# Running sums of a linear attention over pairs of even and odd tokens, five heads in 32 bits and eleven in two halves

## The chip, the cores and the metric
The kernel runs on one core of a Trainium2 chip. TensorE (PE) does the matmuls, VectorE (DVE) and ScalarE (ACT) the work on elements, GpSimd (POOL) small operations and gathers, SyncE (SP) issues most DMA. The metric is the time of one execution on the device in microseconds (us), as a median of several runs.

## What is computed
Two layers on x of 16 sequences, 256 tokens each, 128 wide. Each layer normalises x and adds to it an attention and a feed-forward branch. The first layer has a causal linear attention of 16 heads of width 8 and a mixture of 8 experts, of which each token uses 2. The second has a linear attention without a causal order and a gated feed-forward branch that mixes each token with the one before it. The change concerns mainly the causal attention:

```
def step(carry, qkv):
    K_sum, KV = carry
    q_t, k_t, v_t = qkv
    K_sum = K_sum + k_t
    KV = KV + k_t[..., :, None] * v_t[..., None, :]
    num = jnp.einsum('bhd,bhde->bhe', q_t, KV)
    den = jnp.maximum(jnp.einsum('bhd,bhd->bh', q_t, K_sum), EPS)
    return ((K_sum, KV), num / den[..., None])
```

q and k have gone through a rotation by position and phi(x) = elu(x) + 1. So each token needs, for each head, the sum over all tokens up to it of a product of k (8 numbers) with v and a one (9 numbers): 16 x 9 x 8 = 1152 running sums for a token.

## The kernel before
**Tiles.** A tile is 128 tokens, one on each partition; there are 32, numbered i. A sequence b has two tiles, i = 2b (r = 0, its tokens 0 to 127) and i = 2b + 1 (r = 1, tokens 128 to 255). A sequence is also called a pair here, since it is a pair of tiles.

**The running sums.** `phi` (DVE) makes q and k of a pair. `attn_outer` (DVE) and `attn_keys` (ACT) write the 1152 products of a tile into `outer`. A float32 matmul is slow, so `attn_high` (ACT) rounds the products to a narrower format, `fp32r`, and `attn_low` (DVE) makes the rest; both halves go to PE. `attn_cumsum` (PE) multiplies them with a triangle of ones (`tri_r`), which gives the running sum within the tile; for the second tile of a pair the first tile's products are multiplied with a matrix of ones (`ones_r`) too. The 1152 columns lie in three banks of PSUM, of 5, 5 and 6 heads (360, 360 and 432 columns): 6 matmuls in a first tile, 12 in a second. `attn_apply` (DVE) multiplies the result with q into `cq`, `attn_sums` (DVE) adds over the 8 numbers, and after the second tile `attn_reciprocal` and `attn_divide` (DVE) give y, which PE transposes and projects.

**The order.** Each engine runs its own list of instructions, and semaphores tie them together. The running sums are woven into the 71 steps of the experts: in one step PE transposes the tokens of block j + 2, multiplies the first weights of block j + 1 and the second of block j; ACT takes copies and the gelu. The table `SUMS_AT` gives the step after whose first part the sums of tile i stand on PE: two steps from tile to tile, three at one place, four after the tiles 20 and 25 (`READY_AT`), where DVE also runs `combine` and the second layer's moments for four tiles. One pair has mostly four expert steps. On DVE the order within a tile is written out in `tile`: apply(i), low(i+1), outer(i+2), sums(i), and behind a second tile reciprocal, divide and phi(b+2). So the halves for the next tile are ready before DVE does the sums of this one. POOL gathers the tokens of the expert blocks by indirect DMA (`gather`, six blocks ahead of its count, held back until PE has transposed the block four before), and later the results of the experts (`gather_y`).

**The rest.** Before the experts lie the projections of the first layer (8 groups of four tiles) and the routing. After them comes the second layer in 8 groups of four tiles (`group_tensor`, `group_vector`, ...); in the first five groups DVE also combines the attention's and the experts' results for a later group. `mix` (DVE) adds the token before to each token: columns 0 to 255 of `xT2` to columns 1 to 256.

## Time and profile before
| | |
|---|---|
| median of 3 runs | 368.7 us (367.78 to 368.82) |
| the profiled execution | 367.48 us, of which the span of its instructions is 365.7 us |
| PE busy | 347.7 us (95%) |
| DVE busy | 317.6 us (87%) |
| ACT busy | 276.1 us (75%) |
| POOL busy | 204.3 us (56%) |
| granted clock of PE | 0.999 of full speed |

The profile is of one execution; the time outside its span is 1.8 us. Busy shares are averages over very different stages: the first layer's projections and the routing up to about 68 us, the experts with the running sums up to about 280 us, then the second layer. What binds is read stage by stage.

### The profile page before, as it was taken

The page shows a single profiled execution, that of the slowest core. Times are in us where ns is not written, and L with a number is a line of the kernel's source. Part 1 is how long each engine was busy: PE and PEld are TensorE (multiplying, and loading weights), DVE is VectorE, ACT ScalarE, POOL GpSimd, SP SyncE. Part 2 cuts the span into 40 slices and gives each one's busy share as a digit, 9 for nine tenths or more (in the row PEclk, how much of TensorE's full clock was granted, in tenths as well). Part 3 has the DMA queues.
Part 4 walks back from the last instruction along what each step waited for, and adds up shares of the span by engine and source line. Part 5 has one row for each costly group of instructions (what it writes and reads, how often), then busy time and mean ns, then how long its engine had stood idle before and what let it go on. Part 6 is the DMA issues. An engine that isn't in the chain of part 4 may idle for free.

```text
span 365.7 us, 9318 instructions
## 1 busy us (share of the span) xinstructions
PE 347.7 (95%) x2534; PEld 299.9 (82%) x2534; DVE 317.6 (87%) x623; ACT 276.1 (75%) x774; POOL 204.3 (56%) x239
## 2 busy tenths in 40 slices
PE   7999988799899999999999899999999899999986
PEld 2788534499799999999999799989989688788875
DVE  3998799559989999999699979998996799998665
ACT  3887967777686877787878767787895987778752
POOL 3899118844234465756665648675857448883110
PEclk9999999999999999999999999999999999999999
DMA  6842848555355555655654554756642102221112
GB/s 182 217 124 74 325 192 234 173 149 134 108 133 137 139 143 146 170 139 150 175 143 135 152 161 129 186 150 152 148 115 70 31 2 57 57 61 29 30 29 59
DMA packets 45521, 47.00 MB, mean 129 GB/s; under 512 B 6928, under 2 KB 33712, under 8 KB 45216
## 3 DMA queue, kind: packets, MB, share of 16 engines
q1 hardware_dynamic: 40288, 36.88, 33.6%
q0 software_dynamic: 4320, 8.86, 11.5%
q10 hardware_dynamic: 864, 0.67, 0.7%
q8 instruction: 23, 0.38, 0.5%
q14 instruction: 26, 0.21, 0.2%
HBM read 32.88 MB, written 13.50 MB: 127 GB/s over the span
## 4 chain that ended last, share of the span: by engine, by line
PE 76%; DVE 14%; issue 3%; ACT 3%; DMA 2%; ACTq 1%; DVEq 0%
PE banks L546 16%; PE banks L534 14%; PE banks L674 6%; PE banks L675 6%; PE banks L330 3%; PE banks L983 3%; PE banks L1010 2%; PE banks L299 2%; PE banks L524 2%; PE banks L1039 2%; PE banks L321 2%; PE banks L1019 2%; PE banks L993 2%; PE banks L1057 2%; DVE cq L686 2%
## 5 line engine op out<-in xcount | busy, mean ns | idle before, releaser
L468 POOL DMA_INDIRECT xg<-xn_rows,slot_tok x71 | 74.8, 1053 | 74.2 <-PE banks L524 61.7
L563 ACT ACTIVATE xT<-banks,b1T 128x128 f32<-128x128 f32 x284 | 81.1, 371 | 15.4 <-PE banks L534 14.7
L546 PE MATMUL banks<-w_sb,xT 128*128 x568 | 79.6, 283 | 0.0
L485 POOL DMA_INDIRECT qk_exp<-expert_rows,ranki x64 | 63.7, 996 | 21.6 <-issue 17.9
L534 PE MATMUL banks<-xgT,w 128*128 128x128 f32 x568 | 75.3, 276 | 0.0
L546 PEld LDWEIGHTS banks<-w_sb,xT 128*128 128x128 f32 x568 | 69.3, 192 | 1.2
L534 PEld LDWEIGHTS banks<-xgT,w 128*128 128x128 f32 x568 | 69.0, 192 | 0.0
L686 DVE TENSOR_TENSOR cq<-banks,phi 128x360 f32<-128x360 f32 (+1 forms) x96 | 47.4, 548 | 19.1 <-PE banks L675 18.9
L652 ACT CAST high<-outer 128x1152 fp32r<-128x1152 f32 x32 | 37.1, 1158 | 21.6 <-DVE outer L641 21.2
L658 DVE TENSOR_TENSOR low<-outer,high 128x1152 fp32r<-128x1152 f32 x32 | 43.3, 1352 | 3.2 <-ACT high L652 3.2
L695 DVE TENSOR_REDUCE sums<-cq 128x144 f32<-128x1152 f32 x32 | 42.9, 1341 | 0.0
L641 DVE TENSOR_TENSOR outer<-phi,qkv 128x1024 f32<-128x1024 f32 x32 | 38.7, 1213 | 0.0
L674 PE MATMUL banks<-high,tri_r 128*128 128x360 f32 (+1 forms) x96 | 35.1, 365 | 1.1 <-DVE low L658 1.1
L675 PE MATMUL banks<-low,tri_r 128*128 128x360 f32 (+1 forms) x96 | 32.4, 337 | 0.0
L299 PE MATMUL banks<-zeros_bf 128*128 128x512 bf16 x111 | 28.9, 404 | 1.7 <-DVE zeros_bf L1529 1.0
L291 ACT ACTIVATE xn<-x_sb,shift,rstd 128x128 f32<-128x128 f32 x64 | 26.5, 486 | 0.3 <-POOL shift L279 0.3
L572 ACT COPY ye<-banks 128x128 f32<-128x128 f32 x71 | 19.4, 273 | 9.6 <-PE banks L546 9.1
L524 PE MATMUL banks<-cst,xg 128*128 128x128 f32 x71 | 19.6, 276 | 3.8 <-issue 1.8
L934 POOL TENSOR_TENSOR outer<-outer,x_sb 128x512 f32<-128x512 f32 x7 | 8.9, 1272 | 22.7 <-DVE outer L929 22.6
L555 ACT COPY xgT<-banks 128x128 f32<-128x128 f32 x71 | 19.0, 268 | 3.3 <-PE banks L524 2.5
L299 PEld LDWEIGHTS banks<-zeros_bf 128*128 128x128 bf16 x111 | 10.5, 103 | 12.8 <-issue 2.5
L275 POOL TENSOR_TENSOR rstd<-ve,mhalf 128x4 f32<-128x4 f32 x16 | 19.3, 1207 | 1.3
(205 smaller groups left out, 702.7 us busy)
## 6 DMA issues: line engine op xcount, KB each, us to landing
w<-in_L_ffn_W SPq DMA_DIRECT2D x71, 256.0 KB
expert_rows<-ye SPq DMA_DIRECT2D x71, 64.0 KB
expert_rows<-x_sb SPq DMA_DIRECT2D x2, 2048.0 KB, 10.6
x_sb<-in_L_attn_x SPq DMA_DIRECT2D x8, 256.0 KB, 4.3
xn_rows<-xn SPq DMA_DIRECT2D x8, 256.0 KB, 2.3
w_sb<-in_L_ffn_W SPq DMA_DIRECT2D x8, 256.0 KB, 4.5
out<-outer SPq DMA_DIRECT2D x7, 256.0 KB, 2.3
xg<-xn_rows,slot_tok POOLq DMA_INDIRECT x71
```

Of the source, the lines that this page charges most:

```text
L299: nc.tensor.matmul(ps[bank], zeros_bf[:, :], zeros_bf[:, :].unsqueeze(1).broadcast_to([P, 4, P]), start=True, stop=True)
L468: pool.indirect_dma_start(out=xg[n][:, :], out_offset=None, in_=xn_dram, in_offset=bass.IndirectOffsetOnAxis(ap=slot_tok[:, j:j + 1], axis ...
L485: pool.indirect_dma_start(out=y_moe[:, i, k, :], out_offset=None, in_=y_dram, in_offset=bass.IndirectOffsetOnAxis(ap=ranki[:, 0, k, i:i + ...
L534: last = nc.tensor.matmul(ps[3 + p][:, c * P:(c + 1) * P], w1[n][:, c * P:(c + 1) * P], xgT[p][:, :], start=True, stop=True)
L546: last = nc.tensor.matmul(y, hidT[p][:, c, :], w2_sb[:, ds(e * NC + c, 1), :], start=False, stop=(c == NC - 1))
L563: last = nc.scalar.activation(hidT[p][:, c, :], ps[3 + p][:, c * P:(c + 1) * P], ACT.Gelu_apprx_tanh, bias=b1T[:, ds(e * NC + c, 1)])
L641: nc.vector.tensor_tensor(outer_of(r)[:, :, 0:DH, :], k.unsqueeze(2).broadcast_to([P, H, DH, DH]), vv.unsqueeze(3).broadcast_to([P, H, DH, ...
L658: nc.vector.tensor_tensor(low[n], outer[r], high[n].bitcast(f32), ALU.subtract).then_inc(low_ready, 1)
L674: nc.tensor.matmul(o, w[:, :], high[at][:, cols], start=(m == 0), stop=False)
L675: last = nc.tensor.matmul(o, w[:, :], low[at][:, cols], start=False, stop=(m == len(parts) - 1))
L686: last = nc.vector.tensor_tensor(cq4[:, lo:hi, :, :], ps[n][:, 0:(hi - lo) * E9 * DH].rearrange("p (h e d) -> p h e d", e=E9, d=DH), q[:, ...
L695: nc.vector.tensor_reduce(sums[:, r, :, :], cq4, AX.X, ALU.add).then_inc(sums_ready, 1)
```

## The change
Tokens are laid out differently: partition p of a first tile holds token 2p of its sequence, partition p of a second tile token 2p + 1. The sums over a pair then need only one product of ones and sums of two tokens: DVE adds the products of the two tiles first (`attn_pair`), and only this sum is split and sent to PE. For the odd tokens the triangle includes the diagonal (`tri_r`), for the even ones it doesn't (`tri_x`), and what the even token adds itself is q . k times v, which POOL computes in five operations (`attn_own`) and DVE adds to the sums (`attn_add_own`). The first five heads (360 columns, `whole`) aren't split: they go to PE as one float32 matmul. Loads and stores of tokens now move two neighbouring tokens (1 KB) at a time; `mix` gets four instructions instead of two; in the second layer PE takes the blocks in swapped order (`block_of`). ACT copies three more 128x128 matrices at the start. A few semaphores are shared by the layers, which changes no order.

```
@@ constant_table @@
-        put(name, a.reshape(2, P, DH).transpose(1, 0, 2).reshape(P, -1))
+        put(name, a.reshape(P, -1))
...
+    def by_tile(a, b, n):
+        return a.rearrange("(b p r) d -> p b (r d)", p=P, r=2)[:, b:b + n, :]
+
+    def in_pairs(a):
+        return a.rearrange("p (b r) d -> p b (r d)", r=2)
...
-    high = [sbuf(f"high{n}", [P, HED], f32r)[:, :] for n in range(3)]
-    low = [sbuf(f"low{n}", [P, HED], f32r)[:, :] for n in range(3)]
-
-    def kept(r, p):
-        return 2 if r else p
+    HEADS = ((0, 5), (5, 10), (10, H))
+    WHOLE = HEADS[0][1] * E9 * DH
+    whole = [sbuf(f"whole{n}", [P, WHOLE])[:, :] for n in range(2)]
+    high = [sbuf(f"high{n}", [P, HED - WHOLE], f32r)[:, :] for n in range(2)]
+    low = [sbuf(f"low{n}", [P, HED - WHOLE], f32r)[:, :] for n in range(2)]
...
@@ attn_keys, attn_outer @@
-            act.wait_ge(high_ready, b * 2 - 1 + r)
-            act.wait_ge(low_ready, b * 2 - 1 + r)
+            act.wait_ge(high_ready, b)
+            act.wait_ge(low_ready, b)
+            act.wait_ge(pair_ready, b)
+            act.wait_ge(whole_ready, b)
...
-    def attn_high(act, b, r, p):
-        i = b * 2 + r
-        act.wait_ge(outer_ready, i + 1)
-        act.wait_ge(den_ready, i + 1)
-        if from_(b, 2 - r):
-            act.wait_ge(cum_ps, b * 2 - (0 if r else 2))
-        nc.scalar.copy(high[kept(r, p)], outer[r]).then_inc(high_ready, 1)
-    def attn_low(v, b, r, p):
-        v.wait_ge(high_ready, b * 2 + r + 1)
-        n = kept(r, p)
-        nc.vector.tensor_tensor(low[n], outer[r], high[n].bitcast(f32), ALU.subtract).then_inc(low_ready, 1)
-    HEADS = ((0, 5), (5, 10), (10, H))
+    def attn_pair(v, b, p):
+        v.wait_ge(outer_ready, 2 * b + 2)
+        v.wait_ge(den_ready, 2 * b + 2)
+        if b >= 2:
+            v.wait_ge(cum_ps, 2 * b - 2)
+        nc.vector.tensor_tensor(outer[0][:, WHOLE:], outer[0][:, WHOLE:], outer[1][:, WHOLE:], ALU.add).then_inc(pair_ready, 1)
+        nc.vector.tensor_tensor(whole[p], outer[0][:, 0:WHOLE], outer[1][:, 0:WHOLE], ALU.add).then_inc(whole_ready, 1)
+    def attn_high(act, b, p):
+        act.wait_ge(pair_ready, b + 1)
+        if b >= 2:
+            act.wait_ge(cum_ps, 2 * b - 2)
+        nc.scalar.copy(high[p], outer[0][:, WHOLE:]).then_inc(high_ready, 1)
+    def attn_low(v, b, p):
+        v.wait_ge(high_ready, b + 1)
+        nc.vector.tensor_tensor(low[p], outer[0][:, WHOLE:], high[p].bitcast(f32), ALU.subtract).then_inc(low_ready, 1)
+    def attn_own(pool, b, p):
+        pool.wait_ge(phi_ready, b + 1)
+        if b >= 2:
+            pool.wait_ge(own_used, b - 1)
+        nc.gpsimd.tensor_tensor(own_qk[:, :], phib[p][:, 0, 0:D], phib[p][:, 0, D:2 * D], ALU.mult).then_inc(own_part, 1)
+        q = own_qk[:, :].rearrange("p (h d) -> p h d", d=DH)
+        n = 4 * b + 1
+        for half in (DH // 2, DH // 4):
+            pool.wait_ge(own_part, n)
+            nc.gpsimd.tensor_tensor(q[:, :, 0:half], q[:, :, 0:half], q[:, :, half:2 * half], ALU.add).then_inc(own_part, 1)
+            n += 1
+        pool.wait_ge(own_part, n)
+        nc.gpsimd.tensor_tensor(own_dot[:, :], q[:, :, 0], q[:, :, 1], ALU.add).then_inc(own_part, 1)
+        pool.wait_ge(own_part, n + 1)
+        pool.wait_ge(ones_ready, 1)
+        nc.gpsimd.tensor_tensor(own[p][:, :, :], own_dot[:, :].unsqueeze(2).broadcast_to([P, H, E9]),
+                                qkv3[:, 2 * b, 2 * D:NW].rearrange("p (e h) -> p h e", h=H), ALU.mult).then_inc(own_ready, 1)
+    def attn_add_own(v, b, p):
+        v.wait_ge(own_ready, b + 1)
+        v.wait_ge(sums_ready, 2 * b + 1)
+        nc.vector.tensor_tensor(sums[:, 0, :, :], sums[:, 0, :, :], own[p][:, :, :], ALU.add).then_inc(own_used, 1)
     def attn_cumsum(pe, b, r, p):
...
         i = b * 2 + r
         if from_(i, 1):
             pe.wait_ge(cq_ready, i)
-        pe.wait_ge(low_ready, i + 1)
-        parts = [(tri_r, kept(r, p))] + ([(ones_r, kept(0, p))] if r else [])
+        pe.wait_ge(low_ready, b + 1)
+        pe.wait_ge(whole_ready, b + 1)
+        w = tri_r if r else tri_x
         for n, (lo, hi) in enumerate(HEADS):
             cols = slice(lo * E9 * DH, hi * E9 * DH)
             o = ps[n][:, 0:(hi - lo) * E9 * DH]
-            for m, (w, at) in enumerate(parts):
-                nc.tensor.matmul(o, w[:, :], high[at][:, cols], start=(m == 0), stop=False)
-                last = nc.tensor.matmul(o, w[:, :], low[at][:, cols], start=False, stop=(m == len(parts) - 1))
+            if n == 0:
+                nc.tensor.matmul(o, tri_whole[r][:, :], whole[p], start=True, stop=True)
+                continue
+            cols = slice(cols.start - WHOLE, cols.stop - WHOLE)
+            nc.tensor.matmul(o, w[:, :], high[p][:, cols], start=True, stop=False)
+            last = nc.tensor.matmul(o, w[:, :], low[p][:, cols], start=False, stop=True)
...
@@ attn_reciprocal @@
         v.wait_ge(sums_ready, 2 * b + 2)
+        v.wait_ge(own_used, b + 1)
...
+    OWN_AT = [max(SUMS_AT[2 * b] - 3, 0) for b in range(B)]
...
@@ mix @@
-            t = mix_t[p][m].rearrange("p (b t) -> p b t", t=T)
-            last = nc.vector.scalar_tensor_tensor(out=t, in0=xT2_of(p)[:, :, 0:T], scalar=one_mu[:, m:m + 1],
-                                                  in1=t, op0=ALU.mult, op1=ALU.add)
+            for lo, to in ((P + 1, 0), (0, P)):
+                t = mix_t[p][m].rearrange("p (b t) -> p b t", t=T)[:, :, to:to + P]
+                last = nc.vector.scalar_tensor_tensor(out=t, in0=xT2_of(p)[:, :, lo:lo + P], scalar=one_mu[:, m:m + 1],
+                                                      in1=t, op0=ALU.mult, op1=ALU.add)
...
@@ load_x: save, save_out alike @@
-                sp.dma_start(x_sb[:, tiles, :],
-                             x_in.rearrange("b t d -> (b t) d").rearrange("(n p) d -> p n d", p=P)[:, tiles, :]
+                sp.dma_start(in_pairs(x_sb[:, tiles, :]), by_tile(x_in.rearrange("b t d -> (b t) d"), 2 * g, 2)
...
@@ block.scalar @@
+                    nc.scalar.copy(tri_x[:, :], passing("tri_excl"))
+                    for r, name in enumerate(("tri_excl", "tri_incl")):
+                        nc.scalar.copy(tri_whole[r][:, :], passing(name))
...
+                if i % 2 and i + 1 < NT:
+                    attn_high(act, (i + 1) // 2, (i + 1) // 2 % 2)
...
-                if i + 2 < NT:
-                    attn_keys(act, i // 2 + 1, i % 2, 1 - i // 2 % 2)
-                    attn_high(act, i // 2 + 1, i % 2, 1 - i // 2 % 2)
+                if i % 2 == 0 and i + 2 < NT:
+                    for r in range(2):
+                        attn_keys(act, i // 2 + 1, r, 1 - i // 2 % 2)
...
+            for r in range(2):
+                attn_keys(act, 0, r, 0)
             def first():
-                for r in range(2):
-                    attn_keys(act, 0, r, 0)
-                attn_high(act, 0, 0, 0)
-            def second():
-                attn_high(act, 0, 1, 0)
+                attn_high(act, 0, 0)
...
@@ block.gpsimd @@
+                if j in OWN_AT:
+                    attn_own(pool, OWN_AT.index(j), OWN_AT.index(j) % 2)
...
@@ block.vector, tile @@
-                if i + 1 < NT:
-                    attn_low(v, (i + 1) // 2, (i + 1) % 2, (i + 1) // 2 % 2)
-                if till(b, B - 2):
-                    attn_outer(v, b + 1, r, 1 - p)
-                attn_sums(v, i, r)
-                if r == 1:
+                if r == 0:
+                    if b + 1 < B:
+                        phi(v, b + 1, 1 - p)
+                        for t in range(2):
+                            attn_outer(v, b + 1, t, 1 - p)
+                        attn_pair(v, b + 1, 1 - p)
+                    attn_sums(v, i, r)
+                else:
+                    attn_add_own(v, b, p)
+                    attn_sums(v, i, r)
+                    if b + 1 < B:
+                        attn_low(v, b + 1, 1 - p)
                     attn_reciprocal(v, b)
                     attn_divide(v, b)
-                if r == 1 and till(b, B - 3):
-                    phi(v, b + 2, p)
-            for b in range(2):
-                phi(v, b, b)
+            phi(v, 0, 0)
             for r in range(2):
                 attn_outer(v, 0, r, 0)
-            attn_low(v, 0, 0, 0)
+            attn_pair(v, 0, 0)
+            attn_low(v, 0, 0)
```

What stands in the engines' lists, at two places of the stage with the experts and one on POOL.

DVE, one pair of tiles in the steady part (`cq<-banks,phi` is apply, `low` and `outer` are as above, `sums<-cq` is the reduction, `rden` the reciprocal). Before:

```order
L686 TENSOR_TENSOR cq<-banks,phi 128x360 x2
L686 TENSOR_TENSOR cq<-banks,phi 128x432
L658 TENSOR_TENSOR low<-outer,high 128x1152
L641 TENSOR_TENSOR outer<-phi,qkv 128x16x64
L695 TENSOR_REDUCE sums<-cq 128x144
L686 TENSOR_TENSOR cq<-banks,phi 128x360 x2
L686 TENSOR_TENSOR cq<-banks,phi 128x432
L658 TENSOR_TENSOR low<-outer,high 128x1152
L641 TENSOR_TENSOR outer<-phi,qkv 128x16x64
L695 TENSOR_REDUCE sums<-cq 128x144
L700 RECIPROCAL rden<-sums 128x32
L708 SCALAR_TENSOR_TENSOR y_tok<-rden,sums 128x256
```

In the changed kernel, again from a first tile's apply on (`outer<-outer` is the sum of the tiles' products for eleven heads, `whole<-outer` for five, `sums<-sums,by_turn` adds what the even tokens add themselves):

```order
L742 TENSOR_TENSOR cq<-banks,phi 128x360 x2
L742 TENSOR_TENSOR cq<-banks,phi 128x432
L635 SCALAR_TENSOR_TENSOR phi<-qk_exp,qkv 128x512
L664 TENSOR_TENSOR outer<-phi,qkv 128x16x64 x2
L673 TENSOR_TENSOR outer<-outer 128x792
L674 TENSOR_TENSOR whole<-outer 128x360
L751 TENSOR_REDUCE sums<-cq 128x144
L742 TENSOR_TENSOR cq<-banks,phi 128x360 x2
L742 TENSOR_TENSOR cq<-banks,phi 128x432
L712 TENSOR_TENSOR sums<-sums,by_turn 128x144
L751 TENSOR_REDUCE sums<-cq 128x144
L686 TENSOR_TENSOR low<-outer,high 128x792
```

The two outer products, the pair's sums and phi (which stood behind the division) all stand in the first tile's part; the one split, `low`, stands at the end of the second tile's part, behind its reduction, and is what the next pair's first matmuls wait for.

PE, the running sums of a second tile between the experts' matmuls. Before:

```order
L674 MATMUL banks<-high,tri_r 128x360
L675 MATMUL banks<-low,tri_r 128x360
L674 MATMUL banks<-high,ones_r 128x360
L675 MATMUL banks<-low,ones_r 128x360
L674 MATMUL banks<-high,tri_r 128x360
L675 MATMUL banks<-low,tri_r 128x360
L674 MATMUL banks<-high,ones_r 128x360
L675 MATMUL banks<-low,ones_r 128x360
L674 MATMUL banks<-high,tri_r 128x432
L675 MATMUL banks<-low,tri_r 128x432
L674 MATMUL banks<-high,ones_r 128x432
L675 MATMUL banks<-low,ones_r 128x432
```

In the changed kernel (`tri_whole` is the float32 triangle):

```order
L727 MATMUL banks<-whole,tri_whole 128x360
L730 MATMUL banks<-high,tri_r 128x360
L731 MATMUL banks<-low,tri_r 128x360
L730 MATMUL banks<-high,tri_r 128x432
L731 MATMUL banks<-low,tri_r 128x432
```

Twelve matmuls in fp32r become four, and one in float32 is added; a first tile has the same five with `tri_x` instead of its six.

POOL, in the changed kernel, where before there were only gathers (L487 is the gather of an expert block's tokens):

```order
L487 DMA xg<-xn_rows,slot_tok 128x128 x4
L694 TENSOR_TENSOR own_qk<-phi 128x128
L700 TENSOR_TENSOR own_qk<-own_qk 128x16x4
L700 TENSOR_TENSOR own_qk<-own_qk 128x16x2
L703 TENSOR_TENSOR own_dot<-own_qk 128x16
L706 TENSOR_TENSOR own<-own_dot,qkv 128x144
L487 DMA xg<-xn_rows,slot_tok 128x128 x4
```

The five operations stand behind every fourth gather, one chain for each pair.

## Rows read from the trace of the kernel before
In the first group the columns are the stretch and its length, then the busy us (and the number of instructions) of PE, PEld, DVE, ACT and POOL, PE's granted clock, and the DMA's share and GB/s. In rows in order of time the columns are start, us, engine, line, operation, and in brackets the idle time before and what ended it; x3 means three instructions merged.

**Rows 1.** Windows of 10 us: experts with sums, and second layer.
```profile
110.00:120.00 10.00, 10.00 (x81) 9.45 (x80) 9.67 (x12) 7.54 (x25) 3.99 (x4) 1.00 0.55 147
...
310.00:320.00 10.00, 9.99 (x66) 8.12 (x66) 9.93 (x28) 7.82 (x16) 8.51 (x10) 1.00 0.20 52
```

**Rows 2.** Timeline of PE, running sums of tiles 9 and 10.
```profile
129.79 0.41 PE L674 MATMUL banks<-high,tri_r 128*128 128x360 f32 x1
...
131.97 0.23 PE L544 MATMUL banks<-bias,ones_bf 128*128 x1
...
136.07 0.41 PE L674 MATMUL banks<-high,tri_r 128*128 128x360 f32 x1
...
137.21 0.23 PE L544 MATMUL banks<-bias,ones_bf 128*128 x1
```

**Rows 3.** The chain that ended last: one float32 matmul of 512 columns.
```profile
296.63 0.86 PE banks L1019 x2
```

**Rows 4.** Timeline of DVE, one tile and what follows.
```profile
108.08 1.49 DVE L686 TENSOR_TENSOR cq<-banks,phi 128x360 f32<-128x360 f32 x3 [0.99 <-PE banks L675]
109.49 1.35 DVE L658 TENSOR_TENSOR low<-outer,high 128x1152 fp32r<-128x1152 f32 x1
110.76 1.21 DVE L641 TENSOR_TENSOR outer<-phi,qkv 128x1024 f32<-128x1024 f32 x1
111.89 1.34 DVE L695 TENSOR_REDUCE sums<-cq 128x144 f32<-128x1152 f32 x1
113.27 0.35 DVE L700 RECIPROCAL rden<-sums 128x32 f32<-128x32 f32 x1
...
114.00 0.68 DVE L616 SCALAR_TENSOR_TENSOR phi<-qk_exp,qkv 128x512 f32<-128x512 f32 x1
```

**Rows 5.** Timeline, where DVE and PE wait for each other.
```profile
74.65 0.41 PE L674 MATMUL banks<-high,tri_r 128*128 128x360 f32 x1
...
75.98 1.49 DVE L686 TENSOR_TENSOR cq<-banks,phi 128x360 f32<-128x360 f32 x3 [3.34 <-PE banks L675]
...
91.57 1.35 DVE L658 TENSOR_TENSOR low<-outer,high 128x1152 fp32r<-128x1152 f32 x1
...
93.07 0.40 PE L674 MATMUL banks<-high,tri_r 128*128 128x360 f32 x1 [1.12 <-DVE low L658]
```

**Rows 6.** Timeline of PE, first matmuls of tiles 12 and 30.
```profile
148.12 0.41 PE L674 MATMUL banks<-high,tri_r 128*128 128x360 f32 x1
...
270.53 0.41 PE L674 MATMUL banks<-high,tri_r 128*128 128x360 f32 x1
```

**Rows 7.** Timeline of DVE behind tile 20, combine and moments.
```profile
206.38 2.17 DVE L828 SCALAR_TENSOR_TENSOR x_sb<-qk_exp,sel,x_sb 128x128 f32<-128x128 f32 x8
...
209.49 0.38 DVE L268 BATCH_NORM_AGGREGATE mv<-stats 128x2 f32<-128x6 f32 x4
```

**Rows 8.** Timeline, copies on ACT near the start, and the experts' start.
```profile
16.04 0.30 ACT L1329 CAST tri_r<-cq 128x128 fp32r<-128x128 f32 x1
...
16.24 0.30 ACT L1330 CAST ones_r<-cq 128x128 fp32r<-128x128 f32 x1
...
18.25 1.19 PE L321 MATMUL banks<-w_in,xT 128*128 128x136 f32 x8 [0.64 <-ACT xT L338]
...
70.09 1.15 ACT L652 CAST high<-outer 128x1152 fp32r<-128x1152 f32 x1
```

**Rows 9.** Timeline of POOL and DVE in the second layer.
```profile
306.31 1.27 POOL L934 TENSOR_TENSOR outer<-outer,x_sb 128x512 f32<-128x512 f32 x1
...
307.12 1.03 DVE L888 SCALAR_TENSOR_TENSOR qkv<-qkv 128x512 f32<-128x512 f32 x1
...
309.74 0.20 POOL L277 TENSOR_TENSOR minus<-mv,rstd 128x4 f32<-128x4 f32 x1
...
335.90 0.66 DVE L888 SCALAR_TENSOR_TENSOR qkv<-qkv 128x512 f32<-128x512 f32 x1
```

**Rows 10.** Timeline of DVE, the two instructions of mix.
```profile
311.77 1.44 DVE L880 SCALAR_TENSOR_TENSOR qkv<-qkv,one_mu 128x512 f32<-128x512 f32 x2
```

More of the change, by code:

```diff
@@ L1056, in nd_tensor @@
         for n in range(GT):
[L1057 removed]
+            last = nc.tensor.matmul(nd_bank[:, n, 0:DA], phi_q[:, block_of(n)], kvm[:, n // 2, :],
                                     start=True, stop=True)
@@ L1399, in _ @@
                   even, odd,
-                  first=first, second=second, last=last)
+                  first=first, last=last)
             groups(act, group_scalar)
```

72 lines of the change are left out of this document (40 added, 32 removed).

## The prediction, written before the changed kernel was run
> **What bounds the kernel now.** I read the busy time in stretches first. In the stage of the experts PE has no idle time (10.00 of 10 us) and DVE nearly none (9.67); in the second layer both are full (9.99 and 9.93) [rows 1]. So little is free on two engines, and the question is which chain closes last. The timeline of PE gives the terms of a pair: 2.18 us for the sums of a second tile (129.79 to 131.97), 4.10 for two expert steps (to 136.07), 1.14 for the sums of a first tile (to 137.21) [rows 2]. In this stage PE waits for hardly anything, and what DVE produces is ready before PE asks: PE sets the pace, and DVE is some tenths of a us short of it.
>
> **PE's part.** A float32 matmul of 512 columns takes 0.86 us, recorded in two [rows 3]; for 360 columns that is 0.61. Six fp32r matmuls take 1.14 us for 2 x 1152 columns, so the 720 columns replaced took 0.36, and a tile now costs 1.14 - 0.36 + 0.61 = 1.39 us. A pair costs 2.78 instead of 3.32: PE gains 0.54 of work per pair. This is all that the change can give while PE binds.
>
> **DVE's part.** From the starts in one tile: apply 1.41, low 1.27, outer 1.13, reduction 1.27 (1.34 with its tail); reciprocal and divide 0.73 together, phi 0.68 with its tail [rows 4]. Phi with 512 elements (0.68) and low with 1152 (1.35) give 1.05 ns an element, so 792 elements take 0.97 alone and 0.90 in a row of work, 360 take 0.46, and the 144 of the own part some 0.25. Removed per pair: two lows, 2.54. Added: 0.90 + 0.46 + 0.25 + 0.97 = 2.58. DVE has nothing to gain. What counts is the new order. Low stands last in the second tile's part, PE's next sums wait for it, and the next thing DVE can do beyond reciprocal and divide is the apply that waits for those sums. Before, low stood directly behind apply, and outer and reduction covered PE's sums. Where the two wait for each other, PE starts 0.15 us after low has ended (91.57 + 1.35 to 93.07), and apply starts 1.33 us after the first of six matmuls [rows 5]; with the float32 one this is 1.33 + 0.25 = 1.58.
>
> The loop of one pair, from the first matmul of its first tile to that of the next pair's: sums 1.58, apply 1.41, phi 0.68 (outer waits for its end), outer 1.13 and 1.21 (the sum of the pair waits for the second), pair 0.90, whole 0.46, reduction 1.27, apply 1.41, own 0.25, reduction 1.27, low 0.97, to PE 0.15. Together 12.7 us. PE's own way round is 12.05 - 0.54 = 11.5, where 12.05 is the pair from 136.07 to 148.12 [rows 2, 6]. So the bound moves from PE's work to this loop, 0.65 over the pair of before; DVE stands about 0.85 in it (1.58 less the 0.73 of reciprocal and divide), and PE waits 1.2.
>
> What could break this loop: keys on ACT. They now follow phi by one expert step, after PE has done the first tile's sums, one and a half steps and ACT one copy. By PE's terms that is 1.39 + 2.05 + 2.05 at most, and they end before DVE has done both outers (1.58 + 1.41 + 0.68 + 2.34 = 6.0). The split to high, 0.8 us on ACT, starts at about 7.0 and is needed at about 11.6. Both are hidden.
>
> **The sum over the stage.** Fifteen pairs lie between the first matmuls of tile 0 (74.65) and tile 30 (270.53): 195.9 us [rows 5, 6]. After: twelve at 12.7 = 152.4. Pair 7 has a fifth expert step, and PE binds: 11.5 + 2.05 = 13.6. Pair 12 (extra steps ahead of tile 26) has PE at 11.5 + 4.1 = 15.6, while combine falls into PE's time. Pair 10 has combine and moments inside the loop, 206.38 to 209.87 or 3.5 us [rows 7]: 12.7 + 3.5 = 16.2. Sum 197.8, +1.9 us. The last pair has no follower: PE's 0.5 less, 0.25 for the own part more, -0.25.
>
> **The ends.** Three more 128x128 copies on ACT at the start, 0.20 us each by two neighbours, stand ahead of the xT copy for which PE already waits 0.64: +0.6. At the experts' start the first gelu stands behind the keys and a high of 1.15 us on ACT, and the second behind another; now the keys are done earlier and one high of 0.84 is left [rows 8]. I take -0.7 (0.3 to 1.5).
>
> **POOL's own part.** Five operations per pair, in a stage where POOL only gathered. Where they run beside DVE a row of the second layer shows a price: a DVE instruction with both inputs in SBUF is issued at 307.12 while POOL adds 512 columns (306.31 to 307.58), and takes 1.03 us; with POOL idle the same line takes 0.66 at 335.90 [rows 9]. It gets through when POOL is done, 0.4 later. POOL's small operation takes 0.20 for 4 columns, the large one 1.27 for 512, so the five take about 0.46, 0.33, 0.26, 0.22 and 0.50: 1.8 us. The chain waits for phi, and behind phi DVE has four instructions with two SBUF inputs (outer, outer, pair, whole). If each of the first three POOL operations gets in between two of them and costs its length less 0.1, a pair loses 0.75 us; if POOL's chain falls into applies and reductions, with PSUM or a single input, it loses nothing. I take half, 0.35, as phi is what both wait for but POOL has a gather to issue first. In thirteen pairs in which DVE's loop binds: +4.5 us (0 to 9.8). The Trainium skill, "SBUF — State Buffer", section Who interferes with whom, states the rule: a DVE instruction with two SBUF inputs and a GpSimd instruction that reads SBUF shut each other out for the whole instruction. By that rule the trace's 0.4 us is what is to be expected; taken strictly for all that can meet, the sum would be near its upper end.
>
> **Second layer and DMA.** Two mix instructions of 512 elements take 1.44 us [rows 10]; four of 256 have the same elements and two more fixed parts, 0.68 - 512 x 1.05 ns = 0.14 alone and less in a row: +0.2 per mix. It counts where DVE is full, the first mix and five groups: +1.2. Loads and stores in 1 KB pieces move the same bytes with half the packets; only the first load and the last store aren't covered: -0.2 (0 to -0.6). The swapped blocks change no size.
>
> **Sum.** +1.9 - 0.25 + 0.6 - 0.7 + 4.5 + 1.2 - 0.2 = +7.1 us. The profiled execution took 367.5, so it would take 374.6; it lies 1.2 below the median of the runs shown, within their usual spread, and I add the sum to the median: 375.8 us.
>
> **The rivals.**
> (a) The loop holds, but POOL's chain doesn't meet DVE's: 375.8 - 4.5 = 371.3, range 369.8 to 373.5. For it: applies and reductions, which read PSUM or a single input, are 5.4 of the loop's 12.7 us, and with DVE's wait of 0.85 half of it is free for POOL. Against it: POOL's chain and the outer products both start on phi.
> (b) Faster. PE stays the bound, since DVE's loop is shorter than 12.05 us. Then fifteen pairs at 0.54 less give -8.1, with -0.25 - 0.7 + 0.6 + 1.2 - 0.2 the sum is -7.4: 361.3; with the loop halfway, at 11.8, about 365. The loop would have to be 0.65 shorter than by the rows, a quarter of all that is new on DVE. For it: PE binds now and loses work. Against it: the durations of apply, outer, reduction and low are measured ones.
> (c) About the same: the loop at 12.2 and no meeting: 368.7 +- 1.1.
> (d) POOL costs more, since each operation in the chain of five meets DVE, own part included, or POOL comes late with the gathers of the experts' tokens, which stand in its list between the chains. At 0.7 to 1.0 us a pair instead of 0.35 the thirteen pairs cost 9 to 13 instead of 4.5: 380 to 384. Against it: behind the fourth DVE instruction comes a reduction, beside which POOL is free.
> (e) The change doesn't do what it says: no ground. The list of PE shows five matmuls for six and for twelve.
>
> **Chances.** The forecast, 373.5 to 379.5: 0.45. (a) 0.22. (b) 0.15. (c) 0.08. (d) 0.10. A measurement tells a change of 0.3% (1.1 us). Faster by more: 0.16; within: 0.09; slower by more: 0.75. The range that leaves out (b) and the far end of (d), about 0.2, is 367.5 to 381; the likeliest case alone has 373.5 to 379.5.
>
> **What would show each step.** PE: idle time of about 1.2 us before each first tile's float32 matmul, ended by low, and a float32 matmul of 0.6. DVE: an idle time of about 0.85 before each first tile's apply, ended by PE; in the list of a pair, outer, pair and whole longer than 1.21, 0.97 and 0.46 when POOL's chain runs, if it meets them. A pair of 12.7 to 13.4 from first tile to first tile. ACT: high at about 0.84 and idle before it. The copies and mix at the sizes given. I am wrong if the first tile's matmuls find low ready and PE shows no idle time, or if the pair takes less than 12.05.

## The result, and the profile after

The changed kernel took 380.61 us as a median of four runs (379.66 to 381.1) against 368.56 for the kernel before: a ratio of 1.0327, 95% interval 1.0301 to 1.0354. Forecast were 375.8 us, 367.5 to 381. Sign and mechanism are as forecast, the loss is 12.05 us where 7.1 was written. Ratios are taken between fast executions alone, so they can differ in the third decimal from what the medians give.

First the page of the changed kernel: the busy time of each engine, then some of the costliest groups, each with its number of instructions and, behind the bars, busy us, mean ns of one, and the engine's idle us ahead of them with what ended it.
```profile
PE 341.1 (90%) x2438; PEld 286.7 (76%) x2438; DVE 326.7 (86%) x671; ACT 257.0 (68%) x761; POOL 253.2 (67%) x320
L727 PE MATMUL banks<-whole,tri_whole 128*128 128x360 f32 x64 | 25.6, 482 | 20.5 <-issue 20.5
L742 DVE TENSOR_TENSOR cq<-banks,phi 128x360 f32<-128x360 f32 (+1 forms) x96 | 47.5, 549 | 22.2 <-PE banks L731 20.7
L664 DVE TENSOR_TENSOR outer<-phi,qkv 128x1024 f32<-128x1024 f32 x32 | 41.5, 1336 | 2.0
L700 POOL TENSOR_TENSOR own_qk<-own_qk 128x64 f32<-128x64 f32 (+1 forms) x32 | 24.3, 758 | 2.5
```
PE and DVE, nearly full in the experts' stage before [rows 1], now wait for each other: 20.5 us ahead of the float32 matmuls, 20.7 us ahead of apply. The same stretch as in [rows 1], in windows:
```profile
110.00:120.00 10.00, 8.38 (x66) 7.56 (x66) 8.75 (x16) 5.38 (x18) 4.88 (x6) 1.00 0.38 112
```

One pair in the timeline of PE, DVE, ACT and POOL, from the first matmul of one even tile to that of the next:
```profile
128.59 0.97 DVE L686 TENSOR_TENSOR low<-outer,high 128x792 fp32r<-128x792 f32 x1
129.66 0.84 PE L727 MATMUL banks<-whole,tri_whole 128*128 128x360 f32 x2 [1.49 <-issue]
131.27 1.49 DVE L742 TENSOR_TENSOR cq<-banks,phi 128x360 f32<-128x360 f32 x3 [0.99 <-PE banks L731]
132.67 0.68 DVE L635 SCALAR_TENSOR_TENSOR phi<-qk_exp,qkv 128x512 f32<-128x512 f32 x1
133.49 2.92 DVE L664 TENSOR_TENSOR outer<-phi,qkv 128x1024 f32<-128x1024 f32 x2
133.59 0.47 POOL L694 TENSOR_TENSOR own_qk<-phi 128x128 f32<-128x128 f32 x1
134.14 2.37 POOL L700 TENSOR_TENSOR own_qk<-own_qk 128x64 f32<-128x64 f32 x2
136.44 0.98 DVE L673 TENSOR_TENSOR outer<-outer 128x792 f32<-128x792 f32 x1
136.59 0.92 POOL L703 TENSOR_TENSOR own_dot<-own_qk 128x16 f32<-128x16 f32 x1
137.34 0.55 DVE L674 TENSOR_TENSOR whole<-outer 128x360 f32<-128x360 f32 x1
137.46 0.85 ACT L681 CAST high<-outer 128x792 fp32r<-128x792 f32 x1 [0.71 <-DVE outer L673]
137.82 1.34 DVE L751 TENSOR_REDUCE sums<-cq 128x144 f32<-128x1152 f32 x1
139.26 1.49 DVE L742 TENSOR_TENSOR cq<-banks,phi 128x360 f32<-128x360 f32 x3
140.88 1.34 DVE L751 TENSOR_REDUCE sums<-cq 128x144 f32<-128x1152 f32 x1
142.14 0.97 DVE L686 TENSOR_TENSOR low<-outer,high 128x792 fp32r<-128x792 f32 x1
143.22 0.54 PE L727 MATMUL banks<-whole,tri_whole 128*128 128x360 f32 x1 [1.49 <-issue]
```
The loop closes as forecast: low ends at 143.11 and PE starts 0.11 later, after 1.49 us of idle time. "issue" stands for a wait the profile names no releaser for; low's end tells which, and the run with all heads split below has low by name. The pair takes 13.56 us where 12.7 was forecast, plus 0.35 for the port. POOL's operations lie beside outer, pair and whole, as feared (`by_turn` is the other of the two buffers of `own`).

### The profile page after: what moved, and what is told of

Same layout as the page of the kernel before. It is cut to its first block, busy times and chain, and to the rows that moved or that the text cites. A ratio compares the mean times of both kernels' runs of the same rounds, so it can differ in the third digit from the quotient of the medians.

```text
span 378.5 us, 9362 instructions
## 1 busy us (share of the span) xinstructions
PE 341.1 (90%) x2438; PEld 286.7 (76%) x2438; DVE 326.7 (86%) x671; ACT 257.0 (68%) x761; POOL 253.2 (67%) x320
## 4 chain that ended last, share of the span: by engine, by line
PE 71%; DVE 15%; issue 8%; ACT 3%; DMA 2%; POOL 1%; ACTq 0%; DVEq 0%; POOLq 0%
PE banks L565 17%; PE banks L553 16%; PE banks L727 6%; PE banks L349 3%; PE banks L731 3%; PE banks L730 3%; DVE qkv L944 3%; PE banks L543 2%; PE banks L1074 2%; PE banks L340 2%; PE banks L1103 2%; PE banks L807 2%; PE banks L318 2%; PE banks L1083 2%; PE banks L563 1%
## 5 line engine op out<-in xcount | busy, mean ns | idle before, releaser
L487 POOL DMA_INDIRECT xg<-xn_rows,slot_tok x71 | 72.7, 1024 | 36.1 <-PE banks L543 18.3
L553 PE MATMUL banks<-xgT,w 128*128 128x128 f32 x568 | 76.5, 279 | 0.0
L553 PEld LDWEIGHTS banks<-xgT,w 128*128 128x128 f32 x568 | 70.3, 195 | 0.0
L742 DVE TENSOR_TENSOR cq<-banks,phi 128x360 f32<-128x360 f32 (+1 forms) x96 | 47.5, 549 | 22.2 <-PE banks L731 20.7
L727 PE MATMUL banks<-whole,tri_whole 128*128 128x360 f32 x64 | 25.6, 482 | 20.5 <-issue 20.5
L664 DVE TENSOR_TENSOR outer<-phi,qkv 128x1024 f32<-128x1024 f32 x32 | 41.5, 1336 | 2.0
L727 PEld LDWEIGHTS banks<-whole,tri_whole 128*128 128x128 f32 x64 | 9.6, 190 | 22.6 <-issue 22.6
L700 POOL TENSOR_TENSOR own_qk<-own_qk 128x64 f32<-128x64 f32 (+1 forms) x32 | 24.3, 758 | 2.5
L574 ACT COPY xgT<-banks 128x128 f32<-128x128 f32 x71 | 19.8, 278 | 2.8 <-PE banks L543 1.9
L543 PE MATMUL banks<-cst,xg 128*128 128x128 f32 x71 | 19.6, 275 | 1.7 <-DMA xg<-xn_rows,slot_tok 1.7
L318 PEld LDWEIGHTS banks<-zeros_bf 128*128 128x128 bf16 x111 | 10.5, 103 | 12.8 <-issue 2.5
L1493 POOL TENSOR_SCALAR outer<-xT,token_no 128x144 f16<-128x144 f16 x8 | 8.5, 1104 | 15.9 <-DVE xT L1712 15.8
L886 DVE SCALAR_TENSOR_TENSOR x_sb<-qk_exp,sel,x_sb 128x128 f32<-128x128 f32 x64 | 18.9, 359 | 0.0
## 6 DMA issues: line engine op xcount, KB each, us to landing
expert_rows<-x_sb SPq DMA_DIRECT2D x2, 2048.0 KB, 10.7
```

Source lines behind the costliest of these rows:

```text
L318: nc.tensor.matmul(ps[bank], zeros_bf[:, :], zeros_bf[:, :].unsqueeze(1).broadcast_to([P, 4, P]), start=True, stop=True)
L487: pool.indirect_dma_start(out=xg[n][:, :], out_offset=None, in_=xn_dram, in_offset=bass.IndirectOffsetOnAxis(ap=slot_tok[:, j:j + 1], axis ...
L543: nc.tensor.transpose(ps[6][:, 0:P], xg[n][:, :], ident).then_inc(xgT_ps, 1)
L553: last = nc.tensor.matmul(ps[3 + p][:, c * P:(c + 1) * P], w1[n][:, c * P:(c + 1) * P], xgT[p][:, :], start=True, stop=True)
L664: nc.vector.tensor_tensor(outer_of(r)[:, :, 0:DH, :], k.unsqueeze(2).broadcast_to([P, H, DH, DH]), vv.unsqueeze(3).broadcast_to([P, H, DH, ...
L727: nc.tensor.matmul(o, tri_whole[r][:, :], whole[p], start=True, stop=True)
```

## The experiments

They were run in three sets, each on a chip of its own; the kernel before took 386.1 us in the first, 368.5 in the second and 383.0 in the third. On the first and third chip the records hold stretches of 2 to 5 us in which ACT and DVE start nothing although what they wait for is done, in the changed kernel too. So ratios to the kernel before are compared within a set, and lengths of pairs are read only where no such stretch lies. The changed kernel itself was run again only in the third set. The second set's kernel before took the same 368.5 us as the one of the result, and there I compare with the changed kernel's ratio of 1.0327, though it is from another set of runs.

### First set

**Low first.** Low stands ahead of own and the second reduction.
```diff
+                    if b + 1 < B:
+                        attn_low(v, b + 1, 1 - p)
                     attn_add_own(v, b, p)
                     attn_sums(v, i, r)
-                    if b + 1 < B:
-                        attn_low(v, b + 1, 1 - p)
```


> The changed kernel with low(b+1) ahead of the own part and the reduction of a second tile. Loop theory (PE's sums and DVE wait for each other since low stands last): PE gets its operands about 1.5 us earlier, DVE's wait of 0.87 us ahead of each first tile's apply goes, and the thirteen pairs bound by it shrink from about 13.4 to 12.5 us: 369 to 371 us. Rival (DVE's own work and its meetings with POOL set the pair, the order doesn't matter): 379 to 381 us.

Measured: 409.12 us, ratio 1.0523 (1.0416 to 1.0631). The wait ahead of the float32 matmul fell from 20.5 to 1.0 us, as the loop has it, yet the time was the longest of the set, with 25.6 us of DVE's waiting put down to no engine of this core. Its first pairs, with no stretch of standing still, take 12.4 us (92.78 to 105.21). The run says that low was late, and nothing of what it is worth in the whole; it was repeated below.

**The chain on POOL left out.** It runs for two pairs only; of the others' even tokens the own term is an old one.
```diff
-                if j in OWN_AT:
+                if j in OWN_AT[:2]:
-        v.wait_ge(own_ready, b + 1)
+        v.wait_ge(own_ready, min(b + 1, 2))
```


> The changed kernel in which POOL computes what the even tokens add themselves only for the first two pairs; the later pairs add those old values, so their output is another one. Port theory (POOL's five operations hold up DVE's outer, pair and whole by 0.2 to 0.8 us a pair): outer falls to 1.21 us at its end, pair to 0.97, whole to 0.53, and the time falls by 5 to 6 us to about 375 us. Rival (the longer loop comes from waits between DVE's own instructions, POOL is harmless): 379.5 to 381 us.

Measured: 393.94 us, ratio 1.018 (1.010 to 1.026). An undisturbed pair of it, timeline of DVE:
```profile
117.21 1.49 DVE L742 TENSOR_TENSOR cq<-banks,phi 128x360 f32<-128x360 f32 x3 [0.98 <-PE banks L731]
119.43 2.36 DVE L664 TENSOR_TENSOR outer<-phi,qkv 128x1024 f32<-128x1024 f32 x2
124.61 1.49 DVE L742 TENSOR_TENSOR cq<-banks,phi 128x360 f32<-128x360 f32 x3
130.17 0.97 DVE L742 TENSOR_TENSOR cq<-banks,phi 128x360 f32<-128x360 f32 x2 [0.98 <-PE banks L731]
```
This is the loop without POOL: 12.96 us, and the two outers take 2.36 instead of 2.92, as the port theory has it. The changed kernel's ordinary pairs take 13.23 to 13.55 from apply to apply, so POOL costs 0.27 to 0.59 a pair. The total can't be judged, since the changed kernel wasn't run on this chip.

**The chain later.** It starts one step before the pair's sums instead of three.
```diff
-    OWN_AT = [max(SUMS_AT[2 * b] - 3, 0) for b in range(B)]
+    OWN_AT = [max(SUMS_AT[2 * b] - 1, 0) for b in range(B)]
```


> The changed kernel with POOL's chain two expert steps later in its list, while DVE is in apply and reduction of the second tile. Port theory: the chain meets fewer instructions with two SBUF inputs, but can still meet low, which is on the loop: 375 to 378 us. Rival (POOL harmless): 379.5 to 381 us.

Measured: 396.74 us, ratio 1.0281 (1.0201 to 1.0361); again the total has nothing to be compared with. Its groups by line:
```profile
L664 DVE TENSOR_TENSOR outer<-phi,qkv 128x1024 f32<-128x1024 f32 x32 | 37.8, 1223 | 2.0
L686 DVE TENSOR_TENSOR low<-outer,high 128x792 fp32r<-128x792 f32 x16 | 16.3, 1021 | 1.2 <-ACT high L681 1.2
L674 DVE TENSOR_TENSOR whole<-outer 128x360 f32<-128x360 f32 x16 | 8.4, 525 | 0.0
```
Outer falls from 1336 to 1223 ns and whole from 599 to 525, while low rises from 974 to 1021. The undisturbed pairs take 12.96 to 13.03 (115.87 to 128.89 us for one of them). The meeting at the port is thus a matter of when POOL starts; a small part of the price, 0.05 us a pair, moved to low.

**The ends on the kernel before.** Three copies more on ACT and mix in four instructions.
```diff
+                    for n in range(3):
+                        nc.scalar.copy(low[n][:, 0:P], passing("tri_excl"))
...
-            t = mix_t[p][m].rearrange("p (b t) -> p b t", t=T)
-            last = nc.vector.scalar_tensor_tensor(out=t, in0=xT2_of(p)[:, :, 0:T], scalar=one_mu[:, m:m + 1],
+            for lo in (0, P):
+                t = mix_t[p][m].rearrange("p (b t) -> p b t", t=T)[:, :, lo:lo + P]
+                last = nc.vector.scalar_tensor_tensor(out=t, in0=xT2_of(p)[:, :, lo:lo + P], scalar=one_mu[:, m:m + 1],
...
```


> The kernel before, with three more 128x128 copies on ACT at the start (into buffers that are written later anyway) and mix in four instructions of 256 elements. By the prediction's terms +0.6 and +1.2 (1.5 by the profile of the changed kernel): 370.2 to 370.8 us, with the first gather later by 0.6 and mix at 1.65 us instead of 1.43. Rival (both hidden): 368.6 us.

Measured: 389.16 us, ratio 1.0082 (1.0037 to 1.0127), 1.4 to 4.9 us of 386; forecast were 1.8. PE's wait ahead of its first matmuls of 136 columns shows the copies: 0.64 in [rows 8], 1.24 here and in the changed kernel. Mix takes 1.67 us in four instructions (303.69) where [rows 10] has 1.44 in two. Both are at the size given. The total says less, since in the profiled execution 1.3 us of it stand elsewhere: from the first gathered tokens to the first sums 7.47 us pass where the kernel before has 6.20, with the clock at its lower level.
```profile
18.61 1.19 PE L321 MATMUL banks<-w_in,xT 128*128 128x136 f32 x8 [1.24 <-ACT xT L338]
```

### Second set

**Low first, again.**

> The kernel of e1_low_first once more, on another chip: there it took 5.2% more than the kernel before, with idle stretches of 4 to 5 us in which TensorE, ScalarE and VectorE all stood still among the experts' steps. If those belonged to that chip, the ratio is 0.995 to 1.015 here (low 1.5 us earlier in a pair's loop: 11.9 to 12.5 us a pair); if they belong to the order (rival), it is above 1.03 again and the same stretches are in the trace.

Measured: 378.04 us, ratio 1.0218 (1.0137 to 1.0299). A pair takes 12.43 us (103.86 to 116.29), in the range given; the total gained only some 4 us on the changed kernel's ratio, where 0.995 to 1.015 was expected. So the loop through low is confirmed in the pairs, and the total isn't explained by it; the next run shows where it goes.

**DVE reordered.**
```diff
                 if r == 0:
                     if b + 1 < B:
-                        phi(v, b + 1, 1 - p)
                         for t in range(2):
                             attn_outer(v, b + 1, t, 1 - p)
-                        attn_pair(v, b + 1, 1 - p)
                     attn_sums(v, i, r)
+                    if b + 1 < B:
+                        attn_pair(v, b + 1, 1 - p)
                 else:
+                    if b + 1 < B:
+                        attn_low(v, b + 1, 1 - p)
                     attn_add_own(v, b, p)
                     attn_sums(v, i, r)
-                    if b + 1 < B:
-                        attn_low(v, b + 1, 1 - p)
                     attn_reciprocal(v, b)
                     attn_divide(v, b)
+                    if b + 2 < B:
+                        phi(v, b + 2, p)
-            phi(v, 0, 0)
+            for b in range(2):
+                phi(v, b, b)
```


> The changed kernel with VectorE's work in another order, nothing taken away: tile 0 of a pair is followed by apply, both outer products of the next pair, the reduction, the add over the pair and the whole's add; tile 1 by apply, low, own, reduction, reciprocal, divide and phi of the pair after next. If the loop through low and the sums in waiting order is what the change costs (about 13.2 us for a pair against 11.8 of VectorE's own work), the waits ahead of apply and ahead of the float32 matmul go, pairs take 11.8 to 12.3 us and the time falls by 12 to 20 us against the changed kernel: a ratio to the kernel before of 0.98 to 1.00. If the port shared with GpSimd or the experts' chain on TensorE is the bound (rival), pairs stay above 12.7 and the ratio above 1.015.

Measured: 378.63 us, ratio 1.0274 (1.0205 to 1.0344). Pairs did fall to 11.9 us (103.29 to 115.19; 11.7 to 11.9 in the four behind it), and yet the time hardly moved: both theories missed. Its windows tell why:
```profile
100.00:150.00 50.00, 49.24 (x370) 44.34 (x370) 47.97 (x71) 34.77 (x124) 33.81 (x42) 0.98 0.48 139
150.00:200.00 50.00, 49.78 (x389) 45.30 (x388) 47.94 (x72) 35.73 (x129) 40.19 (x50) 1.00 0.56 154
200.00:250.00 50.00, 43.09 (x324) 39.93 (x323) 39.56 (x72) 29.28 (x108) 40.73 (x45) 0.93 0.47 135
```
Up to 200 us PE is full. From 200 on it is not, and POOL's 40.73 busy us with some 0.3 of issue ahead of each gather fill its 50. The transpose of the gathered tokens (L543) waits, and the timeline of POOL and PE shows for whom:
```profile
227.15 0.94 POOL L487 DMA_INDIRECT xg<-xn_rows,slot_tok  x1 [0.30 <-issue]
228.12 1.17 POOL L694 TENSOR_TENSOR own_qk<-phi 128x128 f32<-128x128 f32 x1
229.36 0.64 POOL L700 TENSOR_TENSOR own_qk<-own_qk 128x64 f32<-128x64 f32 x2
230.08 0.22 POOL L703 TENSOR_TENSOR own_dot<-own_qk 128x16 f32<-128x16 f32 x1
230.38 0.51 POOL L706 TENSOR_TENSOR own<-own_dot,qkv 128x144 f32<-128x144 f32 x1
231.03 0.99 POOL L504 DMA_INDIRECT qk_exp<-expert_rows,ranki  x1
232.33 1.04 POOL L294 TENSOR_TENSOR rstd<-ve,mhalf 128x4 f32<-128x4 f32 x1
233.74 1.05 POOL L298 TENSOR_TENSOR shift<-zero,minus 128x4 f32<-128x4 f32 x1
234.96 1.82 POOL L487 DMA_INDIRECT xg<-xn_rows,slot_tok  x1 [0.16 <-issue]
238.42 0.33 PE L543 MATMUL banks<-cst,xg 128*128 128x128 f32 x1 [3.27 <-DMA xg<-xn_rows,slot_tok]
```
Chain, a gather of results and the moments' operations put 7.8 us between the starts of two gathers of tokens, and PE stands 3.27 us for the second, which it uses 3.5 us after its start. In all PE waits 10.7 us for gathered tokens in 8 waits, 1.7 of them at the experts' start. With low first it is 7.3 us in 5, 1.9 of them there. By apply's starts, tile 0 to 20 and 20 to 30 take 125.3 and 70.9 us before, 134.4 and 73.0 in the changed kernel, 126.1 and 79.4 with low first, 123.2 and 81.8 reordered. What the order gains is given back in the last ten tiles.

**Reordered, chain later.** The edits of both runs above.

> The same order, and GpSimd's own-row chain started one slot before the pair's sums instead of three. Port theory: the chain then lies beside apply, low and reductions that read one operand from a bank, and no longer beside the outer products; 0.3 to 0.5 us less for each of 13 pairs where VectorE bounds, so 3 to 6 us below the run before. Rival (own then comes too late and the second reduction waits for it): level or up to 4 us above it.

Measured: 382.16 us, ratio 1.0369 (1.03 to 1.0438). Outer stays at 1216 ns (median), as in the run before, so there was little left to gain at the port; tile 30 comes 5.6 us later. This is the rival in its direction, but not by its reason: DVE waits nowhere for own. PE waits 10.8 us for gathers in 8 waits, which is as much as in the run before, so it isn't that either. The granted clock was lower (0.973 against 0.986 in the profiled executions); what made it so stays open.

**All heads split.** No float32 sums.
```diff
-    WHOLE = HEADS[0][1] * E9 * DH
+    WHOLE = 0
```


> The changed kernel with no head in 32 bits: all 16 heads' sums of the pair go in two halves, so the whole's add and its 64 float32 matmuls of 0.47 us are gone, the add over the pair and low cover 1152 columns instead of 792 (0.44 us more each). In the loop theory a pair's loop changes by -0.57 (whole) +0.44 +0.44 and about -0.6 on TensorE ahead of apply, so -0.3 us a pair: 374 to 378 us where the changed kernel has 380.3, ratio 1.015 to 1.027. Rival: the float32 matmuls are the change's price (TensorE's time), then the ratio falls to 1.00 or below.

Measured: 382.92 us, ratio 1.0383 (1.0329 to 1.0437). The rival is refuted: the float32 matmuls aren't the price. The ordinary pairs took 13.03 to 13.62, level with the changed kernel or 0.2 shorter, where the loop had 0.3. The one from tile 28 to 30 took 18.0 us (269.97 to 287.98) where the changed kernel has 13.1, about the 5 us by which the total missed: PE waits for gathered tokens there, too (1.0 us at 274.19), and then for ACT, and runs at a granted clock of 0.57 from 280 to 288 us. DVE's low, now the last of the two waits, is named:
```profile
141.91 1.35 DVE L682 TENSOR_TENSOR low<-outer,high 128x1152 fp32r<-128x1152 f32 x1
143.40 0.40 PE L722 MATMUL banks<-high,tri_x 128*128 128x360 f32 x1 [1.14 <-DVE low L682]
```

### Third set

**The changed kernel again.**

> The changed kernel itself beside these three, as their measure: ratio 1.027 to 1.038, first tile to tile 30 207 +- 2 us.

Measured: 404.76 us, ratio 1.0572 (1.0481 to 1.0662): more than on its own chip. Pairs without a stretch of standing still take 13.55 as before (105.81 to 119.36). Tile 0 to tile 30 took 232 us in the profiled execution (409.56 us, the longest of the four), where 205 to 209 were expected; the trace has those stretches in it, and doesn't show their cause.

**Reordered, chain left out.** The order of the reordered run and the edit of the run without the chain.

> e5_reordered with GpSimd's own-row chain left out for all but the first two pairs (the even tokens' own term of the other pairs is then an old one). New theory: three limits lie close to each other. Once VectorE's order no longer waits, pairs take 12.0 to 12.3 us up to 200 us, where TensorE is full; from there GpSimd, which issues a gather in 0.94 us and 0.30 behind it and has the chain of 2.3 us in each pair between them, is late, and TensorE waits for gathered tokens (10.7 us in 8 waits in e5_reordered), with the clock falling to its lower level for stretches. Without the chain GpSimd has 2.5 us more room a pair: the waits for gathers fall below 3 us, and the time by 8 to 14 us against e5_reordered, ratio 0.985 to 1.005. Rival (the chain isn't what makes the gathers late, or the outer products and TensorE bind as well): within 4 us of e5_reordered, ratio above 1.015.

Measured: 379.29 us, ratio 0.9891 (0.9835 to 0.9946), the only one below the kernel before, with the own terms left out. Tiles 0 to 20 and 20 to 30 take 126.1 and 73.4 us, with some of those stretches in both; undisturbed pairs 11.6 to 11.7. PE's waits for gathered tokens fell from 10.7 us in 8 to 2.1 in one, and that one stands at the experts' start: behind it there is none, where the reordered run has 9.1 us. The gathers of 150 to 250 us, first in the reordered run, then here; a first line has the shortest, median and longest in ns and the first and last start, a second one how long, and how often, POOL stood ahead of them until PE had transposed:
```profile
L487 POOL DMA_INDIRECT xg<-xn_rows,slot_tok x32: 941/946/1817, 149.3 to 247.9; - x32
  PE banks L543: 0.9, 3
```
```profile
L487 POOL DMA_INDIRECT xg<-xn_rows,slot_tok x33: 938/943/1728, 149.6 to 249.3; - x33
  PE banks L543: 20.9, 21
```
A gather that waits for PE is early: POOL has 20.9 us to spare here and 0.9 there.

**The chain on DVE.** Nothing left out.
```diff
@@ attn_own: on nc.vector and no longer on nc.gpsimd @@
...
                 else:
                     if b + 1 < B:
                         attn_low(v, b + 1, 1 - p)
+                    attn_own(v, b, p)
                     attn_add_own(v, b, p)
```


> e5_reordered with the chain of five operations on VectorE, behind low, and not on GpSimd; nothing left out. GpSimd's queue is as free as before the change and nobody meets at the port, but VectorE has five more operations of 64 to 144 columns, about 0.9 to 1.1 us a pair by its own small ones: pairs of 12.7 to 13.0 us. Expected 370 to 376 us, ratio 1.005 to 1.02, TensorE's waits for gathers below 3 us. If the chain on GpSimd were free (rival), this would be 10 us or more above e5_reordered.

Measured: 389.3 us, ratio 1.0142 (1.0034 to 1.0251), well under the changed kernel's 1.0572 beside it. The five operations take 1.47 us of DVE (113.47 to 114.94), pairs 13.0, and PE waits 1.7 us for gathers. DVE pays 1.3 us a pair. Whether it is still the better place than POOL isn't shown: the changed kernel beside it differs in the order too, and the reordered one (1.0274, 1.0205 to 1.0344) was run on another chip, with an interval that overlaps this one.

**A warmer start.** Five matmuls of zeros more ahead of the first gathered tokens.
```diff
-                keep_warm(2 if g + 1 < NG else 20, 0)
+                keep_warm(2 if g + 1 < NG else 25, 0)
```


> The changed kernel with five more matmuls of zeros ahead of the first gathered tokens (25 instead of 20), so that TensorE idles 0.2 us and not 1.23 there. If the fall of the granted clock to 0.51 at 70 to 72 us comes behind this idle time and took back the 0.7 us that was forecast for the experts' start, the eight matmuls of a step take 1.06 to 1.12 us there and not 1.67 and 1.92, and tile 0's first sums start at 74.2 +- 0.4 instead of 75.25; the whole time 0.5 to 1.5 us shorter than the changed kernel's beside it. Rival (the clock falls whatever stands ahead): no change.

Measured: 406.28 us, ratio 1.0554 (1.0443 to 1.0665), level with the changed kernel beside it. Windows of this kernel, and of the changed one beside it, whose experts start 1.2 us later:
```profile
70.00:72.00 2.00, 2.00 (x17) 1.92 (x18) 0.65 (x1) 1.56 (x5) 1.39 (x3) 1.00 0.15 35
72.00:74.00 2.00, 1.57 (x14) 1.34 (x14) 0.34 (x1) 1.65 (x8) 1.70 (x2) 1.00 0.68 177
```
```profile
72.00:74.00 2.00, 2.00 (x13) 1.96 (x12) 0.98 (x1) 1.78 (x6) 1.52 (x2) 0.59 0.27 61
74.00:76.00 2.00, 2.00 (x13) 1.98 (x11) 0.00 (x0) 0.75 (x3) 1.67 (x3) 0.56 0.50 172
```
The clock held, the eight matmuls take 1.13 and 1.06 us, and from the first gathered tokens to the first sums it took 5.66 us and not 6.49. That is 0.8 us, too little for the total to tell. The first sums start at 74.88, later than the 74.2 +- 0.4 given, as PE still stood 0.64 us for the tokens. That the five matmuls held the clock isn't shown: it held without them, too, in four other profiled executions (see below).

## Why the prediction was right in sign and short in size

The kernel before had 125.3 + 70.9 us; the rows below are of the profiled executions, 380.34 against 367.48.

| term | forecast | measured |
|---|---|---|
| copies at the start, at the first gathered tokens | +0.6 | +0.3 |
| experts' start, from there to the first sums | -0.7 | +0.3 |
| stage, first matmul of tile 0 to tile 30, without port | +1.9 | +5.2 |
| six small instructions on DVE in the first pair | none | +0.5 |
| port | +4.5 | +5.7 |
| last pair | -0.25 | -0.7 |
| second layer | +1.2 | +1.6 |
| last store | -0.2 | -0.1 |
| sum | +7.1 | +12.8 |

The measured column is read between these starts, before and after: first gathered tokens on PE 68.45 and 68.77, first sums 74.65 and 75.25, sums of tile 30 270.53 and 282.58, first projection of the second layer 283.48 and 294.87, DVE's last instructions 362.40 and 375.40, end of the span 365.7 and 378.5. Of the 0.6 us that the copies add to PE's wait at 18 us, 0.3 are left at the first gathered tokens.

**The bound moves from PE to the loop: right.** The signs named are there: PE's wait ahead of each first tile (1.49 us, forecast 1.2), DVE's ahead of apply (0.98, forecast 0.85), five matmuls of a tile in 1.34 to 1.41 us (forecast 1.39). That the waits through low are what lengthens a pair is shown by low first (12.43 us) and by the other order (11.9), with nothing taken away in either.

**The loop was mis-sized, 12.7 for 12.96.** Its durations hold, three joints don't. "Phi 0.68 (outer waits for its end)": from phi's start to outer's 0.82 pass. "Reduction 1.27": where apply waits for the reduction's end, 1.44 pass (in the run without the chain, 123.17 to 124.61). The two outers with the pair's sum behind them take 2.39, not 2.34. I took the distance of most instructions from a row of instructions that wait for nothing, where the next one starts about 0.08 ahead of the end; with a wait for the engine's own previous instruction it starts 0.03 to 0.14 behind it. [rows 4] had such a joint: from the reduction's start to the reciprocal's 1.38 pass. Over thirteen pairs this is 3.4 us, the largest part of the 5.7 that I was short.

**POOL's port: right in kind, 5.7 for 4.5.** Against 12.96, thirteen pairs lost 0.1 to 1.1 us each from apply to apply, 6.2 together. Of the first pair's 1.1 some 0.5 isn't the port: between divide and the next apply DVE has six small instructions for the experts' weights (89.27 to 90.82), which the sum left out and which the kernel before has too. That leaves 5.7, or 0.44 in the mean for 0.35 forecast. That it is the port is shown by the chain left out (12.96) and the chain later (12.96 to 13.03). DVE's outers lose 0.56, POOL's two adds take 2.37 instead of 0.64 us: both wait, POOL longer. The Trainium skill, "SBUF — State Buffer", section Who interferes with whom, has a DVE instruction with two SBUF inputs and a GpSimd instruction that reads SBUF shut each other out; the trace agrees in that both lengthen, and what DVE lost in a pair (0.44) stayed far under the 1.82 us that the chain takes alone (74.21 on).

**Pairs 7 and 12: right** (13.4 and 15.8 for 13.6 and 15.6). Pair 10 took 17.2, forecast 16.2: its loop, and the chain, which there met combine (3.22 us for the 2.17 of [rows 7]).

**Experts' start: the gain was made and taken back.** In the changed kernel PE idles 1.23 us and 0.45 before the first transposes, the granted clock then falls from 1.00 to 0.51, the lower level of 1.2 GHz:
```profile
70.00:72.00 2.00, 2.00 (x12) 2.00 (x12) 0.98 (x1) 1.40 (x5) 1.39 (x3) 0.51 0.16 39
72.00:74.00 2.00, 2.00 (x13) 1.94 (x13) 0.00 (x0) 1.39 (x7) 1.70 (x2) 0.64 0.72 171
```
Eight matmuls take 1.92 us there instead of 1.06. From first gathered tokens to first sums it is 6.20 before, 6.48 after, and 5.55 to 5.66 in the four runs with the change whose clock held (chain later, reordered, all split, warmer start): 0.6 less, the forecast 0.7. The idle time alone doesn't decide. Of the 14 profiled executions the clock held in five, behind 0.64 to 1.68 us (the kernel before with 1.48 is one), and fell in nine, behind 1.23 to 3.35.

**What I saw and put aside: POOL's queue.** "In a stage where POOL only gathered" was read as free time; that gathers could come late stands in rival (d) alone, with half a sentence and no price of its own. The gathers of 150 to 250 us, first in the kernel before, then in the changed one:
```profile
L468 POOL DMA_INDIRECT xg<-xn_rows,slot_tok x34: 938/944/1173, 150.8 to 248.4; - x34
  PE banks L524: 23.0, 15
```
```profile
L487 POOL DMA_INDIRECT xg<-xn_rows,slot_tok x32: 938/945/1437, 152.2 to 247.7; - x32
  PE banks L543: 1.0, 2
```
They wait 23.0 us for PE before and 1.0 in the changed kernel. So the new limit stood right behind the loop and didn't cost the changed kernel anything yet (behind the first sums PE waits for no gathered tokens), since its loop was slower still; that is why shortening the loop by 1.6 us a pair brought 2 us and not 20. The cause is shown by the chain left out of the reordered kernel, where PE's waits behind the start are gone. How much of the ratio's fall from 1.027 to 0.989 is this and how much the chip stays open, as the two ran on different ones.

No kernel that computes everything was faster than the one before.

## What to carry to other kernels

Add up a loop across engines from starts, and where an instruction waits for the one before it on its own engine, take the distance from a row where one waits, too: here it was 0.1 to 0.2 us more than in a row without waits, twice or more in each pass. Before work is put on an engine that looks half idle, read what its queue is waiting for: a gather that waits for its consumer has slack, and one that is issued back to back has none. If shortening the first limit brings nothing, look at the stage in parts: the time may have been gained in one and given back in the next.
